# An audio tower on one core: the second eight batches of V stored by themselves, the third group's rows loaded before the other stores, q of groups two and three issued by ScalarE

## The reference

```python
h = signature(x) @ tok_W.T + tok_b            # path signature to depth 4, 128 features
y = layernorm(h)                              # attention ("lambda layer"), in blocks
q = bn(y @ Wq + bq)   # seen as [block, head 8, DK 16, t]
k = softmax(y @ Wk + bk, over t)
v = bn(y @ Wv + bv)   # seen as [block, DK 16, t]
lam_c = einsum('bukt,buvt->bkv', k, v)
lam_p = relu(conv3x3(v, Wpos))                # over the (v, t) plane, padding 1
h = h + (q . lam_c + q . lam_p) @ Wout + bout
h = h + top1_experts(layernorm(h)) + shared_ffn(layernorm(h))   # 8 experts, I = 512
```

## Time and profile before

| | us |
|---|---|
| median of 3 runs | 637.65 |
| lowest, highest | 637.46, 639.41 |
| the profiled execution | 638.09 |
| its span, from the first to the last instruction | 636.1 |
| mean granted TensorE clock of the profiled execution | 0.975 of full speed |

### The profile page before, as it was taken

How to read it: one execution, slowest core, us unless ns; L and a number is a source line. 1 busy time by engine, 2 the same in 40 slices (tenths; PEclk the granted TensorE clock), 3 DMA queues, 4 the chain that set the end, 5 groups by cost and what they waited for, 6 DMA issues and landing times. The chain is left out here.

```text
span 636.1 us, 13527 instructions
## 1 busy us (share of the span) xinstructions
PE 587.9 (92%) x3737; PEld 469.5 (74%) x3737; DVE 501.1 (79%) x1407; ACT 278.7 (44%) x693; POOL 304.1 (48%) x307
## 2 busy tenths in 40 slices
PE   2789999999999999999895999999999899999993
PEld 0467888888888888888663677777777678888882
DVE  6968889999999988887764788988788677777772
ACT  3332233333333332331224667676767745555541
POOL 3924334555544443320033468887767553333332
PEclk9798999999999999999998899999999999999997
DMA  8402455566665544555655545554441322222210
GB/s 285 45 1 86 153 180 179 187 196 201 202 188 184 163 145 154 163 168 169 154 125 168 126 102 135 126 130 103 112 106 46 93 77 80 74 59 76 60 32 1
DMA packets 127171, 80.02 MB, mean 126 GB/s; under 512 B 66548, under 2 KB 121485, under 8 KB 127126
## 3 DMA queue, kind: packets, MB, share of 16 engines
q1 hardware_dynamic: 122642, 72.89, 40.7%
q0 software_dynamic: 3296, 6.27, 3.1%
q10 hardware_dynamic: 1188, 0.30, 0.2%
HBM read 30.64 MB, written 49.33 MB: 126 GB/s over the span
## 5 line engine op out<-in xcount | busy, mean ns | idle before, releaser
L1251 DVE SCALAR_TENSOR_TENSOR P<-PS,QN 128x512 f32<-128x512 f32 x128 | 79.5, 683 | 26.3 <-PE PS L1430 25.7
L553 DVE SCALAR_TENSOR_TENSOR Z<-PS,Vt,Z 126x128 f32<-126x128 f32 x224 | 78.6, 351 | 8.6 <-PE PS L681 0.6
L681 PE MATMUL PS<-Wh,Ah 128*126 128x512 f32 x256 | 79.6, 434 | 0.0
L339 POOL TENSOR_TENSOR INCl<-INC,INCh 126x512 fp32r<-126x512 f32 x31 | 40.1, 1293 | 76.4 <-ACT INCh L416 76.4
L681 PE MATMUL PS<-Wl,Ah 128*126 128x512 f32 x256 | 71.9, 404 | 2.9 <-DVE Wl L517 2.9
L793 POOL DMA_INDIRECT out_h<-LC,KVH x39 | 38.0, 973 | 73.4 <-DVE LC L837 72.8
L681 PE MATMUL PS<-Wh,Al 128*126 128x512 f32 x256 | 70.7, 397 | 0.0
L681 PEld LDWEIGHTS PS<-Wl,Ah 128*126 128x126 f32 x256 | 48.8, 191 | 15.7 <-issue 3.3
L855 PE MATMUL PS<-W1h,IM 128*128 x156 | 58.7, 416 | 1.0 <-issue 1.0
L681 PEld LDWEIGHTS PS<-Wh,Al 128*126 128x126 f32 x256 | 48.3, 189 | 12.6
L456 ACT ACTIVATE XT<-PS 128x126 f32<-128x126 f32 x32 | 8.9, 277 | 108.0 <-PE PS L729 108.0
(11 more groups left out here) (230 smaller groups left out, 1480.3 us busy)
## 6 DMA issues: line engine op xcount, KB each, us to landing
routed<-nobody SPq DMA_DIRECT2D x30, 1170.0 KB, 5.3
IM<-v_pad SPq DMA_DIRECT2D x124, 72.0 KB
KVH<-routed SPq DMA_DIRECT2D x39, 130.0 KB, 2.2
WRW<-in_w SPq DMA_DIRECT2D x16, 256.0 KB, 3.1
R<-h_rows SPq DMA_DIRECT2D x16, 129.9 KB
W1l<-in_wsig SPq DMA_DIRECT2D x4, 512.0 KB, 8.8
WR<-in_w SPq DMA_DIRECT2D x8, 256.0 KB, 3.2
q_raw<-QS SPq DMA_DIRECT2D x32, 63.0 KB
```

Of the source, the lines that this page charges most:

```text
L339: pool.tensor_tensor(INCl[:], INC[:], INCh[:].bitcast(f32), ALU.subtract).then_inc(incl_ready, 1)
L553: ins = dve.scalar_tensor_tensor(Z[:, u], psU[h][:, d], sc, Z[:, u], ALU.mult, ALU.add)
L681: ins = pe.matmul(out, a, w, start=(n == 0), stop=(n == len(turn) - 1))
L1251: ins = dve.scalar_tensor_tensor(P[:, b, HV * h:HV * h + HV], psC[2 * pair + hb], 0.0, QN[:, g % 2, b:b + 1].broadcast_to([128, HV, SP]), ...
```

## The change

Five edits, all in `middle`:

1. Store 1 (sequences 8 to 15, that is groups 2 and 3) gets a semaphore of its own, `v1_stored`. SyncE issues it after group 0's rows are in, and ahead of group 1's rows.
2. After group 1's rows and `load_h(0)` SyncE waits for `v1_stored` and for `conv_done` 4, and loads group 2's rows there, ahead of the stores 2 to 7.
3. `load_h(1)` and `load_w2(0)` change places behind the stores 2 and 3.
4. The wait for the six stores 2 to 7 moves into the loop, ahead of group 4's rows (k = 2). Group 3's rows (k = 1) have only store 1 to wait for.
5. `load_q` is a function of `middle` now. SyncE loads q of group 0 alone ahead of `pat_q`; ScalarE issues the loads for groups 1 and 2, behind its Exp table load (L1119).

```diff
+        def load_q(eng, g):
+            src = q_raw.rearrange("(b s) f -> b (s f)", b=NB)[g * GB:g * GB + GB, :].rearrange("b (p s) -> p b s", p=128)
+            eng.dma_start(QR[:, g % QB], src).then_inc(q_in[g % QB], 16)
...
-            for g in range(QB):
-                load_q(g)
+            load_q(sp, 0)
...
             sp.wait_ge(v_ready, 2)
-            store_v(0)
+            store_v(0, v0_stored)
             sp.wait_ge(pat, 16)
             sp.dma_start(PQ[:], bass.AP(pat_q.tensor, 0, [[S, 128], [64 * F, 2], [1, S]])).then_inc(pat, 16)
             sp.wait_ge(v0_stored, 16)
             load_im(sp, 0, (0,))
             for pair in range(2):
                 sp.wait_ge(im_in[0][pair], 64)
+            sp.wait_ge(v_ready, 4)
+            store_v(1, v1_stored)
             load_im(sp, 1)
             load_h(0)
-            sp.wait_ge(v_ready, 4)
-            for q in range(1, 4):
-                store_v(q)
+            sp.wait_ge(v1_stored, 16)
+            sp.wait_ge(conv_done, 4)
+            load_im(sp, 2)
+            for q in (2, 3):
+                store_v(q, v_stored)
+            load_w2(0)
             load_h(1)
-            load_w2(0)
             sp.wait_ge(v_ready, 6)
             for q in range(4, G8):
-                store_v(q)
+                store_v(q, v_stored)
             load_w2(1)
-            sp.wait_ge(v_stored, 16 * (G8 - 1))
             for k in range(NG):
                 if on(k + 2, QB, NG):
                     wait_from_one(sp, qn_ready, k)
-                    load_q(k + 2)
-                if on(k + 2, 0, NG):
+                    load_q(sp, k + 2)
+                if on(k + 2, 3, NG):
                     sp.wait_ge(conv_done, 4 * k + 4)
+                    if k == 2:
+                        sp.wait_ge(v_stored, 16 * (G8 - 2))
                     load_im(sp, k + 2)
...
             act.activation(probe[:, 0:1], eps[0:1], ACT.Exp)
+            for g in range(1, QB):
+                load_q(act, g)
             act.wait_ge(ks_ready, 1)
```

More of the change, by code:

```diff
@@ L946, in middle @@
         ks_ready, exp_done, w36_k_ready, v_ready, vn_ready = sem("ks_ready"), sem("exp_done"), sem("w36_k_ready"), sem("v_ready"), sem("vn_ready")
-        v0_stored, v_stored, kv_done, kvt_ready = sem("v0_stored"), sem("v_stored"), sem("kv_done"), sem("kvt_ready")
+        v0_stored, v1_stored, v_stored, kv_done, kvt_ready = sem("v0_stored"), sem("v1_stored"), sem("v_stored"), sem("kv_done"), sem("kvt_ready")
         im_in, q_in = [[sem(f"im_in{n}{p}") for p in range(2)] for n in range(2)], [sem(f"q_in{n}") for n in range(QB)]
@@ L997, in _ @@
         def _(sp):
-            def load_q(g):
-                src = q_raw.rearrange("(b s) f -> b (s f)", b=NB)[g * GB:g * GB + GB, :].rearrange("b (p s) -> p b s", p=128)
-                sp.dma_start(QR[:, g % QB], src).then_inc(q_in[g % QB], 16)
             def load_h(g):
@@ L1019, in _, with store_v @@
                          BNR[:].unsqueeze(1).broadcast_to([64, 2, F])).then_inc(pat, 16)
-            def store_v(q):
-                sp.dma_start(v_pad[8 * q:8 * q + 8, 1:DK + 1], VC[:, q].rearrange("p c s -> p (c s)").bitcast(f32)).then_inc(v_stored if q else v0_stored, 16)
+            def store_v(q, done):
+                sp.dma_start(v_pad[8 * q:8 * q + 8, 1:DK + 1], VC[:, q].rearrange("p c s -> p (c s)").bitcast(f32)).then_inc(done, 16)
             sp.wait_ge(v_ready, 2)
-            store_v(0)
+            store_v(0, v0_stored)
             sp.wait_ge(pat, 16)
```

## The result

| | before | changed |
|---|---|---|
| median of 16 runs, us | 636.89 | 634.81 |
| lowest, highest, us | 634.48, 639.58 | 629.72, 639.40 |
| the profiled execution, us | 638.09 | 634.59 |
| its span, us | 636.1 | 632.6 |
| mean granted clock of the profiled execution | 0.975 | 0.979 |

A forecast was written before the change was run, and what follows sets the result against it. TensorE, busy 92% of the span, was taken as the bound, so time comes out where it stands still. 5.47 + 3.70 + 0.25 - 1.15 - 0.50 = 7.8 us, giving a median of 629.8 us, range 628.2 to 633.0.

The forecast's parts named there:

- Group 2's rows ahead of the stores: At group 2's first convolution, TensorE's wait for rows queued behind seven stores would go: 5.47 us gained.
- Step 2 at a normal pace: From group 2's first convolution to group 3's, the clock would not fall: 10.20 us instead of 13.90, 3.70 us gained.
- The rival of the falling clock: Small pauses in steps 1 and 2 lower the clock all the same; step 2 keeps 13.9 us: 633.5 us, chance 0.05.
- Store 1 ahead of group 1's rows: Before group 1's convolutions, 192 KB more in the queue would make rows that were just in time late: 1.15 us lost.
- Group 3's q and rows: In step 2, these loads queue behind the stores; q lands near 349.9 and delays QN and X2l: 0.5 us lost.
- Start: At the second block's start, two q loads fewer on SyncE let store 0 go earlier: 0.25 us gained.

The follow-up runs named there:

- e4: The kernel before with 22 unused matmuls in its wait for group 2's rows, the wait itself kept; ratio 0.9995.
- e1: The changed kernel with store 1 behind group 1's rows instead of ahead of them; ratio 0.9911 to the kernel before.
- e2: The changed kernel with the q loads of all three groups back on SyncE's queue; ratio 0.9950 to the kernel before.
- e9: As e1, with group 3's q and rows, residual rows and weights also ahead of the stores 2 to 7; ratio 0.9885 to the kernel before.
- e12: The changed kernel run again unaltered, beside the filled one on the same chip; ratio 0.9936 to the kernel before.
- filled kernel: The changed kernel with ten unused matmuls in step 1, six ahead of group 1's second pair, four ahead of group 0's transposes; ratios 0.9873 and 0.9878.
- e7: The changed kernel with q of all three groups on SyncE and ten unused matmuls in step 1; ratio 0.9896 to the kernel before.
- e6: The kernel before with four unused matmuls ahead of group 0's transposes in step 1 and 22 in the wait for group 2's rows; ratio 0.9972.
- e3: First run of the filled kernel: the changed kernel with ten unused matmuls in the pauses of step 1; ratio 0.9873 to the kernel before.
- e11: The filled kernel run again, on another chip beside the changed kernel; ratio 0.9878 to the kernel before.
- e10: As e9, with four unused matmuls ahead of group 0's transposes in step 1; ratio 0.9849 to the kernel before.
- e8: The changed kernel with only four unused matmuls ahead of group 0's transposes in step 1; ratio 0.9932 to the kernel before.

## Why the prediction was wrong, point by point

- **Group 2's rows ahead of the stores, 5.47 us: right.** They were issued at 331.19, 19.6 us after the block's start (my 331.3 is 18.1, so they went 1.5 us later than I had; the eight loads of group 1 took 4.71 us to issue behind store 1, not 3.3), and no convolution of group 2 waited in any profile of the changed order.
- **Step 2 at a normal pace, 3.70 us: this is the step that failed.** "Without the stand-still nothing makes the clock fall: step 1 ran at 1.00" took one execution for the rule. A pause of about 1 us in step 1 can bring the clock down or not: it did not in the profile of before, it did in the profile of e4, which is the same order of transfers. The clock fell in step 1 in all five profiles of the changed orders without filling matmuls (the changed kernel, e1, e2, e9, e12). Of the 28 executions of the changed kernel (16 and 12), four had a mean clock of 0.986 and took 629.4 to 629.9 us, on my forecast; the others had 0.965 to 0.981. Of the ten of the filled kernel all were at 0.984 or more, though not all of e7's were. In the profiles group 4 comes 5.4 us (57.39 against 51.99) and 5.7 us (57.68 against 51.99) later with the fall than without.
- **The rival of the falling clock** had a chance of 0.05 and a price of 3.7 us. It happens in most executions, as far as the profiles and the mean clocks tell, and costs 5.4 to 5.7 us in each of the two profiled ones; over all executions 3.7 us remain (0.9936 against 0.9878 of 637.4). That this equals the 3.70 us priced is chance: that price was read from step 2 of the kernel before, and the fall in the changed kernel slows step 1 as well as step 2. Its cause was named, small pauses in steps 1 and 2, and dismissed with the one row that spoke against it. The Trainium skill, "TensorE: Matmul & The Clock Gate", section "A second HAM failure mode: psum-queue depth-cycling", says that frequent short idles can throttle the engine. The changed kernel's windows agree (busy 0.50, 1.62, 1.93 and 0.97 of 2 us from 331 to 339, then 0.50 of the clock); in e1 the fall came within a single pause of 0.90 us.
- **Why a fall costs the changed kernel more than the kernel before.** Before, a fall in step 1 made TensorE late for rows that were later still. The change took that wait away and with it the cover. I had asked of each edit what hides it, but not what the removed wait had been hiding. e4's profile shows the cover at work (step 1 ended 2.9 us later and still ahead of the rows). The ratios point the same way: e4 and e6 gained 0.0005 and 0.0028 in the order of before, the filling gained 0.0058 in the changed one (0.9936 to 0.9878). They do not prove it, since e4's matmuls delayed group 2, e6 did not hold the clock, and the intervals are wide for such differences.
- **The 3.70 us had two causes.** 1.33 us of it was the second pair's own wait, and e6 took 13.67 us for step 2 with the clock at 1.00 at its start. The sum 5.47 + 3.70 was right as a sum, since rows in time remove both; the second number was read as the clock's alone.
- **Store 1 ahead of group 1's rows, 1.15 us: too small.** The second pair came at 21.79 instead of 19.98 us after the block's start, 1.8 us later where the sum has 0.9, and group 2 2.1 us later than with store 1 behind (31.19 against 29.07). It also made a pause where there was none, which the sum had not priced at all, and by e2 that pause alone can bring the clock down.
- **Group 3's q and rows, 0.5 us: right in place, too large.** q was there 36.75 us after the block's start in the filled kernel (my 36.7), with 0.45 us to spare, since everything ahead was later by the 1 us just named. The two errors cancel in part: 1.0 us too little there, 0.5 too much here.
- **Start, 0.25 us:** store 0 was issued 0.34 us earlier and landed 4.10 us later instead of 4.01; worth nothing (e7).
- **The sum with the clock held.** It puts group 4 at 59.22 - 7.8 = 51.42 us; the profiles with the clock held have 51.99, 51.99, 51.95 and 51.66, so in place the gain was 7.2 us in the filled kernel, the store's and the start's terms having been too kind and group 3's too harsh. As a time: 7.8 forecast, 8.1 and 7.8 measured by the ratios 0.9873 and 0.9878 (7.9 and 7.5 by the medians); that close an agreement is partly luck. The order of transfers was read rightly, the clock was not.

Not settled: what decides in which executions a pause of 1 us brings the clock down. The runs show that it varies, and that with both pauses filled it did not happen in steps 1 to 3 of the three profiles taken (e3, e7, e11). A mean clock counts falls anywhere in an execution, so how often each pause is to blame stays open too.

## What to carry to other kernels

A long wait for a transfer covers whatever is slow just before it, the clock above all. Before pricing its removal, list the pauses of TensorE ahead of it, and take one profile with the clock at 1.00 as a sample and not as a rule; look at the mean clocks of several executions. When such a wait is removed, fill the pauses that it had covered, in the same change: here ten unused matmuls nearly doubled the gain (0.9936 to 0.9878 on one chip), and with the transfers reordered for one more group the ratio was 0.9849, in an interval that overlaps the former.

## What the hardware showed that was not expected

- Pauses of about 1 us stood ahead of a fall in some executions: the clock fell in a single pause of 0.90 us (e1, busy 1.11 of 2 us in 335 to 337), and in e10 some 2 us after one of 0.90 us at the first rows.
- A pause and the fall behind it are not tied: 1.11 of 2 us busy in 337 to 339 left the clock at 1.00 in the profile of before, 1.33 of 2 us in 335 to 337 was followed by the fall in e4. In e2 the clock fell during the 1.59 us ahead of group 1's second pair; 1.51 us at the same place in e8 left it at 1.00.
- The same program took from 629.4 to 638.4 us on one chip (e12), roughly in the order of its mean clock; five executions of the filled one took 628.2 to 630.3.
- Under the backlog SyncE's issuing slows: group 3's eight row loads took 6.65 us to issue, 3.30 with an empty queue.
